# Sheaf edge loop: ten more edge columns summed on TensorE, and first-layer matmuls over 32 rows in pairs

## What is computed

```python
def reflection(a, b):
    h = relu(concatenate([a, b], axis=1) @ W1.T + b1)      # 32 -> 64
    return h @ W2.T + b2                                   # 64 -> 16
F_s, F_d = householder(reflection(xs, xd)), householder(reflection(xd, xs))
L_sd = -einsum('eki,ekj->eij', F_s, F_d)
# L_sd is applied to the end nodes' features; the products, weighted by the
# degrees, are summed into the rows of each edge's source and destination
```

## Time and profile before

| | |
|---|---|
| median of three runs | 23530.96 us |
| profiled execution, first to last instruction (span) | 23516.1 us |
| the median minus this span | 14.9 us |
| TensorE matmul busy | 18959.3 us (81%) |
| VectorE busy | 13526.5 us (58%) |
| GpSimd busy | 17392.8 us (74%) |
| mean granted TensorE clock, share of 2.4 GHz | 0.882 |

### The profile page before, as it was taken

How to read it: one execution, slowest core, us unless ns; L and a number is a source line. 1 busy time by engine, 2 the same in 40 slices (tenths; PEclk the granted TensorE clock), 3 DMA queues, 4 the chain that set the end, 5 groups by cost and what they waited for, 6 DMA issues and landing times. The chain is left out here.

```text
span 23516.1 us, 304821 instructions
## 1 busy us (share of the span) xinstructions
PE 18959.3 (81%) x105910; PEld 12094.2 (51%) x105910; DVE 13526.5 (58%) x25320; ACT 2368.9 (10%) x5716; POOL 17392.8 (74%) x15021
## 2 busy tenths in 40 slices
PE   0688882789995388888888888679999998899997
PEld 0344441344442255555555555367777765555556
DVE  2788883455554266666556555445555552677772
ACT  0000000000000011111111111011111111111111
POOL 5777774777775788888888888478888880777775
PEclk9888885899997688888888888779999997999998
DMA  2222221112121111111222111123333321788884
GB/s 96 51 61 61 61 60 20 40 42 47 41 47 27 27 32 32 32 32 32 35 37 36 32 32 30 30 53 47 52 49 48 50 34 54 236 251 251 250 250 127
DMA packets 1968267, 1657.06 MB, mean 70 GB/s; under 512 B 780455, under 2 KB 1732934, under 8 KB 1949718
## 3 DMA queue, kind: packets, MB, share of 16 engines
q0 software_dynamic: 889216, 465.71, 14.3%
q10 hardware_dynamic: 821300, 579.22, 7.9%
q1 hardware_dynamic: 256354, 594.03, 7.5%
HBM read 953.63 MB, written 684.18 MB: 70 GB/s over the span
## 5 line engine op out<-in xcount | busy, mean ns | idle before, releaser
L1347 PE MATMUL node_sums<-placed_row,lane_values 128*128 128x392 bf16 x34500 | 6165.9, 338 | 534.3 <-DVE placed_row L1335 534.3
L1405 POOL DMA_INDIRECT acc<-column_sums,sum_rows x3375 | 5663.3, 1678 | 1193.1 <-issue 1140.1
L803 POOL DMA_INDIRECT gathered<-gat_table,src_index x4810 | 4835.3, 1005 | 1496.3 <-issue 1471.0
L1347 PEld LDWEIGHTS node_sums<-placed_row,lane_values 128*128 128x128 bf16 x34500 | 3455.8, 102 | 2962.7 <-DVE placed_row L1335 557.2
L1626 POOL DMA_INDIRECT gathered<-sheaf_table,src_index x3125 | 3402.1, 1089 | 960.2 <-issue 942.9
L2409 POOL DMA_INDIRECT gathered<-message_table,src_index x2381 | 2362.0, 992 | 727.5 <-issue 725.1
L1010 PE MATMUL lanes_ps<-S,table_parts 128*128 128x512 bf16 x9828 | 2272.4, 394 | 334.3 <-DVE S L875 334.3
L1335 DVE TENSOR_SCALAR placed_row<-iota_rows_f,src_row 128x1568 bf16<-128x1568 f16 x2875 | 1799.7, 651 | 1119.5 <-PE node_sums L1347 1090.3
L1010 PE MATMUL lanes_ps<-code_onehot,table_parts 128*128 128x512 bf16 x9828 | 2210.5, 386 | 154.7 <-DVE code_onehot L875 154.5
L1010 PEld LDWEIGHTS lanes_ps<-S,table_parts 128*128 128x128 bf16 x9828 | 985.3, 102 | 1558.3 <-DVE S L875 320.3
L1010 PEld LDWEIGHTS lanes_ps<-code_onehot,table_parts 128*128 128x128 bf16 x9828 | 972.5, 100 | 1332.3 <-DVE code_onehot L875 161.9
(11 more groups left out here) (484 smaller groups left out, 22192.5 us busy)
## 6 DMA issues: line engine op xcount, KB each, us to landing
message_rows<-gathered ACTq DMA_DIRECT2D x250, 1600.0 KB, 11.4
src_rows<-src_rows SPq DMA_DIRECT2D x200, 640.0 KB
src_rows<-src_rows SPq DMA_DIRECT2D x125, 960.0 KB
code_rows<-src_code_rows SPq DMA_DIRECT2D x360, 256.0 KB, 3.3
gat_rows<-scanned ACTq DMA_DIRECT2D x25, 3375.0 KB
gathered<-gat_table,src_index POOLq DMA_INDIRECT x4810
acc<-column_sums,sum_rows POOLq DMA_INDIRECT x3375, 3.1
gat_rows<-scanned ACTq DMA_DIRECT2D x25, 2125.0 KB, 6.8
```

What stands on the lines that cost most here:

```text
L803: g.indirect_dma_start(G[b][:, j, :], None, tab, bass.IndirectOffsetOnAxis(ap=IX[b][:, j:j + 1], axis=0)).then_inc(s_g[b], 16)
L1347: last = pe.matmul(o.acc[:, m, 0:Q8 // 4], lane, o.OW[r][:, m * (Q8 // 4):(m + 1) * (Q8 // 4)], start=first(k, 1) and i == 0 and part == 0 ...
L1405: g.indirect_dma_start(self.acc[i], bass.IndirectOffsetOnAxis(ap=o.IXS[b][:, j:j + 1], axis=0), o.SV[b][:, j, :], None, compute_op=ALU.add ...
```

## The change

`MT` goes from 70 to 80, so 45 columns of a chunk are scattered and 80 summed on TensorE. The ten additional columns (`sum_tiles`) are summed between the equality sums, at most one after a group. On TensorE, four of the five column sums of a group q move between the halves of the two layers; the first-layer matmuls take only the 32 partitions of their column, and two of them stand next to one another. VectorE makes a tile's `lane_values` when its first column comes up (`place`), keeps the bf16 parts in a buffer of their own, moves the output scans between the equality matrices, and makes the first two of these before the stretch begins. The source rows that are compared are stored as int16 (also in layer 2). `lane_values` has 4 buffers, not 5.

```diff
-MT = 70
+MT = 80
+TAIL = 10
...
-        self.src_rows = self.dram("src_rows", (EP, P))
+        self.src_rows = self.dram("src_rows", (EP, P), I16)
...
-        o.ROW = [sb(f"src_rows{b}", [P, width * ACCS, P]) for b in range(2)]
+        o.ROW = [sb(f"src_rows{b}", [P, width * ACCS, P], I16) for b in range(2)]
...
-            self.tile_buffers(c, o, MT, [...], (MT - SG * ACCS) // ACCS - 1,
+            self.tile_buffers(c, o, MT, [...], 4,
...
-            late_tiles = range(SG * ACCS, MT - 2 * ACCS)
-            last_tiles = range(MT - 2 * ACCS, MT)
+            late_tiles = range(SG * ACCS, MT - 2 * TAIL)
+            sum_tiles = range(MT - 2 * TAIL, MT - TAIL)
+            last_tiles = range(MT - TAIL, MT)
+            beside = [sum_tiles[g * len(sum_tiles) // o.sums:(g + 1) * len(sum_tiles) // o.sums] for g in range(o.sums)]
...
+            SCANS = [range((g - 2) * D // 12, (g - 1) * D // 12) if 2 <= g < 14 else range(0) for g in range(o.sums)]
...
-                            if not first(k, 1):
-                                for i in tiles[q]:
-                                    self.tile_sum(pe, o, k - 1, 1 - b, i)
-                                if q == 0:
-                                    pe.wait_ge(o.s_sv, k * o.sums)
+
+                            def tile(i):
+                                if not first(k, 1):
+                                    self.tile_sum(pe, o, k - 1, 1 - b, tiles[q][i])
+                            tile(0)
+                            if not first(k, 1) and q == 0:
+                                pe.wait_ge(o.s_sv, k * o.sums)
...
-                            for j in range(4):
-                                n = q * 4 + j
-                                if not first(k, 1) or n >= 2:
-                                    pe.wait_ge(s_r, k * (4 * SG) + (n - 1))
-                                pe.matmul(pre[j % 2][:], W1z[:, j, :], XT[:], start=True, stop=True).then_inc(s_pre, 1)
-                                if j:
-                                    second(j - 1)
-                            second(3)
+                            for half in range(2):
+                                for j in (2 * half, 2 * half + 1):
+                                    n = q * 4 + j
+                                    if not first(k, 1) or n >= 2:
+                                        pe.wait_ge(s_r, k * (4 * SG) + (n - 1))
+                                    rows = slice(2 * D * j, 2 * D * (j + 1))
+                                    pe.matmul(pre[j % 2][:], W1z[rows, j, :], XT[rows, :], start=True, stop=True).then_inc(s_pre, 1)
+                                tile(1 + 2 * half)
+                                second(2 * half)
+                                second(2 * half + 1)
+                                tile(2 + 2 * half)
...
                             last.then_inc(o.s_sum, 1)
+                            if not first(k, 1):
+                                for i in beside[g]:
+                                    self.tile_sum(pe, o, k - 1, 1 - b, i)
...
-                        if not first(k, 1):
-                            self.lane_values(v, o, k - 1, 1 - b, MT // ACCS - 1, parts)
                         w(v.reciprocal(n2[:], n2[:]))
...
                         w(v.tensor_tensor(Q[:, :, 0:D], Q[:, :, 0:D], XX[:, :, D:2 * D], ALU.add))
-                        late(1)
+                        late(3)
+                        for g in range(o.nq):
+                            self.equal(v, o, k, b, g)
...
+                        for g in range(o.sums):
+                            if g == 0:
+                                w(v.tensor_tensor(VP, ...))
+                            if g == 1:
+                                w(v.tensor_tensor(Q[:, :, D:2 * D], Q[:, :, D:2 * D], bcast(NP_.unsqueeze(2), [P, CH, D]), ALU.mult))
...
+                            for f in SCANS[g]:
+                                ins = v.tensor_tensor_scan(OUT[b][:, :, f], sm, Q[:, :, D + f], ...)
...
+                            if not first(k, 1):
+                                place(beside[g])
+                            if g + o.nq < o.sums:
+                                self.equal(v, o, k, b, g + o.nq)
+                        if not first(k, 1):
+                            place(last_tiles[:ACCS])
+                            self.lane_values(v, o, k - 1, 1 - b, last_tiles[ACCS] // ACCS, parts)
+                            v.wait_ge(o.s_svh, k * (MT // ACCS))
                         self.lanes(v, w, o)
```

More of the change, by code:

```diff
@@ L21 @@
 I32 = mybir.dt.int32
+I16 = mybir.dt.int16
 BF16 = mybir.dt.bfloat16
@@ L258, in setup @@
             s_g2, s_g3 = self.dsem("samples_in"), self.dsem("edges_in")
-            turned = [sb(f"src_turned{i}", [P, P], F32, c) for i in range(2)]
+            turned = [sb(f"src_turned{i}", [P, P], I16, c) for i in range(2)]
             turned16 = [sb(f"src_code_turned{i}", [P, 2, P], F16, c) for i in range(2)]
@@ L1560, in sheaf_edges @@
             o = self.scatter_buffers(c, SC, 2, 2)
+            assert o.sums == 16 and TAIL == 2 * ACCS and (MT - TAIL) % ACCS == 0 and MT - 2 * TAIL > (SG + 1) * ACCS
             flat = Q[:].rearrange("p c f -> p (c f)")
-            self.tile_buffers(c, o, MT, [sb(f"placed_row{i}", [P, Q8], BF16)[:] for i in range(ACCS)], (MT - SG * ACCS) // ACCS - 1,
+            self.tile_buffers(c, o, MT, [sb(f"placed_row{i}", [P, Q8], BF16)[:] for i in range(ACCS)], 4,
                               V[:].rearrange("p c f -> p (c f)")[:, 0:Q8])
@@ L1759, in ahead, with place @@
                         def ahead(q):
-                            for t in opens[q]:
-                                self.lane_values(v, o, k - 1, 1 - b, t, parts)
-                            for i in tiles[q] if q < SG else range(SG * ACCS, (SG + 1) * ACCS):
+                            place(range(q * ACCS, (q + 1) * ACCS))
+                        def place(columns):
+                            for i in columns:
+                                if i % ACCS == 0:
+                                    self.lane_values(v, o, k - 1, 1 - b, i // ACCS, parts)
                                 self.onehot_dve(v, o, k - 1, 1 - b, i)
@@ L1768, in late @@
                             if not first(k, 1):
-                                for i in range(at[0], min(at[0] + n, MT - 2 * ACCS)):
-                                    self.onehot_dve(v, o, k - 1, 1 - b, i)
+                                place(range(at[0], min(at[0] + n, late_tiles[-1] + 1)))
                                 at[0] += n
@@ L1805, in compute @@
                         w(v.tensor_tensor(Q[:, :, 0:D], V[:, 0:CH, 0:D], XX[:, :, D:2 * D], ALU.mult))
-                        late(1)
+                        late(2)
                         w(v.tensor_tensor(Q[:, :, D:2 * D], V[:, 0:CH, D:2 * D], XX[:, :, 0:D], ALU.mult))
-                        late(1)
+                        late(2)
                         w(v.tensor_reduce(tt[:], pair(Q[:]), AX.X, ALU.add))
@@ L1821, in compute @@
                         v.sem_inc(s_val, 1)
-                        late(2)
-                        w(v.tensor_tensor(VP, Q[:, SC:CH, 0:D], bcast(DP[:, SC:CH].unsqueeze(2), [P, MT, D]), ALU.mult))
-                        late(1)
-                        self.lanes(v, w, o)
-                        w(v.tensor_tensor(Q[:, :, D:2 * D], Q[:, :, D:2 * D], bcast(NP_.unsqueeze(2), [P, CH, D]), ALU.mult))
-                        late(2)
-                        if not first(k, 2):
-                            v.wait_ge(s_o[b], m - 16)
@@ L1830, in compute @@
-                        for f in range(D):
-                            ins = v.tensor_tensor_scan(OUT[b][:, :, f], sm, Q[:, :, D + f], OUT[1 - b][:, CH - 1, f:f + 1], ALU.mult, ALU.add)
-                        w(ins)
-                        assert at[0] >= MT - 2 * ACCS or first(k, 1)
-                        v.sem_inc(s_done, 1)
-                        for g in range(o.sums):
-                            self.equal(v, o, k, b, g)
-                        if not first(k, 1):
-                            for i in last_tiles[:ACCS]:
-                                self.onehot_dve(v, o, k - 1, 1 - b, i)
+                        assert at[0] > late_tiles[-1] or first(k, 1)
```

24 lines of the change are left out of this document (13 added, 11 removed).

## The result

The changed kernel takes 23383.72 us (median of four runs, 23354.98 to 23397.71) where the kernel before, run beside it, takes 23529.51 us: a ratio of 0.9937, 95% interval 0.9925 to 0.9949. It is faster by 0.63%; the forecast was slower, 23610 us. The time lies inside the range, and within 14 us of rival 1.

The account below looks back on a forecast made before the run. GpSimd was taken to bound the kernel at 284.5 us a chunk, then TensorE and VectorE at 286.4; 46 + 14 + 8 + 20 - 5 = +83 us on the 23516.1 us span, plus 14.9, forecast as 23610 us, range 23350 to 23870.

Parts of the forecast that it names:

- rival 1: Faster: the equality-sum stretch keeps its clock and pairs overlap more; ring 276.4 us, about 23370 us; 0.3 with a whole-overlap case.
- GpSimd's ring: GpSimd's gathers and scatter-adds per chunk: ten scatter-adds fewer shorten 284.5 us to a floor of 264.6 us.
- 138.4 + 54 + 62 + 32: TensorE's and VectorE's chunk: loop over q, to s_val, equality sums with ten columns, to next transposes; 286.4 us.
- the pair's: Loop over q: two neighbouring 32-row first-layer matmuls take three steps for four passes, gaining 0.43 us, 0.14 net.
- 0.29 us for going in and out: Loop over q: cost per pair of changing between full and small matmuls, taken from a layer 3 row.
- 18.1 with no overlap: Loop over q: slow bound of a group's time in us, if the two matmuls of a pair gain nothing.
- the 16.4 us: Loop over q: a group's time with whole overlap of pairs, named as a sign that the forecast is wrong.
- Rival 3: Slower by much: the clock stays low beside the equality sums, 75 us there; ring 302.6 us, 24000 us; chance 0.12.
- Rival 4: Nothing changes: the ring comes out between 282 and 285 us, 23530 us; chance 0.2.
- Rival 5: 32-row matmuls run as before plus 0.29 us a pair; ring 293 us, 23770 us; part of the slower cases.
- Rival 2: GpSimd's saving comes in full: ring 264.6 us, about 23110 us; chance 0.03.
- -5 was forecast: Chunk 0: its equality sums start before its scans while the gathers nearly bound it; 5 us less.

Follow-up runs that it names:

- experiment 3: The changed kernel with both matmuls of a pair on the rows and weights of the pair's first column; ratio 1.0072 to the kernel before, 23726.13 us.
- experiment 1: The changed kernel with its first-layer matmuls over all 128 rows again, same places and order; ratio 1.0018 to the kernel before, 23620.15 us.
- Experiment 9: The changed kernel with ten columns in one block, VectorE's later work spread, and 128-row first-layer matmuls in chunk 0 alone; ratio 0.9851, 23217.24 us.
- experiment 6: The changed kernel with four equality-matrix buffers for two and two lane buffers for four; ratio 0.9942 to the kernel before, 23368.18 us.
- experiments 8: The changed kernel with the ten columns in one block behind the equality sums and VectorE's work after it spread; ratio 0.9878, 23210.38 us.
- experiment 2: The changed kernel with a column sum between the two 32-row matmuls of a pair; ratio 1.0229 to the kernel before, 24092.85 us.

## Why the prediction went wrong

**What was right.** GpSimd's ring stops being the bound, and the wait of L1753 goes. In the sum 138.4 + 54 + 62 + 32 three of four terms hold: 51.6, 62.3 and 31.7 us in chunk 9, 51.6, 60.9 and 33.8 on average. That the 62 came so near is luck in part: it was a value chosen between 50 and 79 us, not one worked out. The drain and the last chunk were put at +28 us (+29 by their terms, as the last chunk's add up to +9 and not +8); from the last chunk's first transposes to the last column sum it is 410.4 us before and 424.7 after, +14, and of the 14 us missing 9 are the shorter groups. Chunk 1 was +14, measured +11 (272 to 283 us between first transposes). The int16 rows brought nothing in layer 2, as forecast: from the last column sum to the end of the program it is 8443 us before and 8444 after.

**The step that failed** is the pair's: "both passes of a column need the same rows, so I take three steps for four passes: 0.43 us gained". The four passes take two steps: the first passes of the two columns start 7 ns apart, then the two second ones. That gains 0.86 us, the bound that I had named and not taken. The cost against it, 0.29 us for going in and out, was right to the hundredth (experiment 3: 0.20 + 0.09). A pair gains 0.57 us by these terms; by the average starts from chunk 3 on it gains 0.55. The second fault in the same step is the order: I gave the column sum that hides the ReLU 0.1 us, from one short wait in the earlier trace rows, and experiment 1 shows 0.45 us a group for the order alone, of which 0.25 us are waits for the ReLU between first-layer passes over the whole group, 0.17 us the second layer's 32 passes (3.58 us in small lots, 3.41 us in two of 16) and 0.03 us the transposes. 17.68 - 2 x 0.55 - 0.45 = 16.13 us, and measured is 16.12 in the median. Over eight groups the two faults are 9.4 us, from 286.4 to 277.0 us, which turns +2.1 a chunk into -7.4; measured is -8.2. (The bound "18.1 with no overlap" adds up to 18.2, which moves the slow end of the range by some 15 us.) A group under the 16.4 us that the forecast had named as a sign of being wrong is what the trace shows.

The Trainium skill (TensorE: Matmul & The Clock Gate, Part 3, The mechanism) states that matmuls in different row groups run concurrently. This case agrees with it: 1.06 us for two on different rows in the changed kernel, 1.91 us for two on the same in experiment 3. By the bound with a whole overlap I had 16.4 us a group, nearer than my own 17.3. The Trainium skill (TensorEngine Tiling (Array Packing), Key Properties) also states that changing the tiling mode drains the engine. That agrees with the 0.29 us for going in and out, though no run separates a drain from other causes of them.

**The rivals.** Rival 1 came in by its first case: I gave it a ring of 276.4 and 23370 us, measured are 276.2 and 23384. That the numbers agree so well is luck: its stretch of 56 us did not come, the stretch was 61 to 62, and the groups were 16.1 and not 16.8. Rival 3 is half there: the granted clock in the stretch was 0.75, between its 0.50 and the 1.00 of layer 2. Rival 4, no change, lies outside the interval. Rival 5 is excluded by the pair's 1.06 us against the 1.71 of experiment 1. Rival 2 is closed by the floor of 268.9 us.

**The time.** Between the first transposes of chunk 2 and of chunk 24 the time falls by 182.5 us (22 x -8.3), chunk 1 gives +11.2, chunk 0 +19.8 (200.3 for 180.5 us), what lies before chunk 0's transposes +14.6 and what follows chunk 24's +15.1: together -121.8 us, and the spans differ by 121.7. Chunk 0 is the other term of wrong sign: -5 was forecast, with the floor of its gathers in mind. Experiment 9 shows what was missed, the clock of the pairs where no column sums stand beside them. The 15 us before chunk 0 can't be put down to the change: the first scans of chunk 0 start anywhere between 7773 and 7876 us in profiles of kernels whose code before that point is the same or nearly so.

**What stays open.** The clock still swings within the stretch of the equality sums after its first column, and no run separates whether TensorE's short waits for one-hots or the mixture with the equality sums brings it down there. In experiment 6 the lane ring was changed too, and VectorE's waits stayed in good part. Why the matmuls over 32 rows go with a lower granted clock, no run shows. And the times of experiments 8 and 9 are not told apart.

## What to carry to other kernels

Where a bound from a row and a rule name both ends of a term, and the sum's sign depends on where between them the value lies, put the forecast's chance there: here 0.43 us a pair decided between faster and slower. Here the float32 matmuls of 512 columns on different row groups gained only next to one another; one alone between full ones was slower than the full one. And where two engines' rings are within a few per cent of one another, look at what the second allows before shortening the first: the two halves of this change were each worth 0 or less, and only together 0.6%.

## What the runs showed of the hardware

Two float32 matmuls of 512 columns over 32 different rows each: 1.06 us, over the same rows 1.91 us, full ones 1.71 us, one alone 1.05 us (float32, all at a granted clock of 1.00). A matmul over 32 rows alone between full ones is here dearer than the full one it replaces (0.86 us). The granted clock was lower with first-layer matmuls over 32 rows than with the same ones over 128: 0.50 against 0.82 in chunk 0, and in experiment 2 a fall to 0.51 about once a group in a loop that had stood at 1.00. The equality matrices made from int16 rows were no faster for VectorE: 827 ns for 826.
